# Second gate-up product on VectorE, a load per convolution tap, and a reordered first chunk in a state-space and mixture-of-experts layer

## The reference

```python
h = layernorm(x)
xc, z = split(h @ in_proj_w.T)                    # 2 x 512
u = causal_conv(xc, conv_w) + conv_b              # 4 taps, 512 -> 512 channels
dt = clip(sigmoid(u @ dt_w.T + dt_b), 1e-4, 1.0)
B, C = u @ B_w.T, u @ C_w.T                       # 16 states
state = exp(clip(dt * -exp(A_log), -5, 5)) * state + dt * B * u + 1e-6   # over time
y = sum(state * C) + D * u
x = x + (y * silu(z)) @ out_w.T
h = layernorm(x)
# top 2 of 8 experts by softmax(h @ gate_w.T), weights normalised over the two
x = x + sum_over_picked(w_e * ((silu(h @ Wg_e) * (h @ Wu_e)) @ Wd_e)) \
      + sigmoid(h @ shared_gate) * (silu(h @ Sg) * (h @ Su)) @ Sd       # hidden width 352
```

## Time and profile before

| | us |
|---|---|
| median of 3 runs | 3082.39 |
| lowest and highest | 3077.94, 3083.76 |
| the profiled execution, device time | 3076.53 |
| its span in the trace | 3074.5 |
| busy: TensorE / GpSimd / VectorE / ScalarE | 2651.9 / 2462.9 / 2131.7 / 2115.1 |

### The profile page before, as it was taken

The page is one execution under the profiler, slowest core; times in us unless marked ns, Lnnn a source line. Parts: engine busy times, 40 slices in busy tenths (PEclk is TensorE's granted clock), DMA queues, the critical chain, the costliest instruction groups (busy, mean ns, idle before and its releaser), DMA issues. The chain is left out here.

```text
span 3074.5 us, 57196 instructions
## 1 busy us (share of the span) xinstructions
PE 2651.9 (86%) x15616; PEld 2307.9 (75%) x15616; DVE 2131.7 (69%) x4576; ACT 2115.1 (69%) x4987; POOL 2462.9 (80%) x1667
## 2 busy tenths in 40 slices
PE   6788888898888888988988888889876699999997
PEld 4677877787777777877877777788765577777776
DVE  1889889889888998899899888998894111111111
ACT  1878888888887888888888887888783233333332
POOL 1989999989998999999899988999993365656555
PEclk9889989989988899899898898898987899999999
DMA  3222222223222222222222222222220677777775
GB/s 134 99 70 80 80 73 80 74 75 97 81 77 75 89 73 85 77 74 81 74 79 98 75 76 74 89 74 87 70 70 21 171 184 180 184 177 185 178 184 126
DMA packets 136253, 309.91 MB, mean 101 GB/s; under 512 B 14992, under 2 KB 79632, under 8 KB 135696
## 3 DMA queue, kind: packets, MB, share of 16 engines
q1 hardware_dynamic: 108880, 270.03, 28.0%
q0 software_dynamic: 27072, 36.46, 6.1%
HBM read 258.42 MB, written 48.01 MB: 100 GB/s over the span
## 5 line engine op out<-in xcount | busy, mean ns | idle before, releaser
L1023 POOL TENSOR_TENSOR room<-dtu,b_all 128x1024 f32<-128x1024 f32 x512 | 1202.8, 2368 | 13.3 <-POOL dtu L1000 5.9
L809 ACT ACTIVATE bank<-room,eps_col 128x512 f32<-128x512 f32 x1024 | 693.8, 684 | 309.2 <-DVE carry L1261 213.2
L796 ACT ACTIVATE room<-room,neg_a 128x256 f32<-128x256 f32 x2048 | 868.5, 499 | 9.6 <-DVE room L1247 7.6
L604 PE MATMUL bank<-ident,room 128*128 128x128 f32 x4096 | 556.7, 293 | 239.2 <-DVE room L1256 201.3
L604 PEld LDWEIGHTS bank<-ident,room 128*128 128x128 f32 x4096 | 501.7, 152 | 293.5 <-DVE room L1256 219.5
L1247 DVE TENSOR_TENSOR_SCAN bank<-room,carry,bank 128x256 f32<-128x256 f32 x864 | 580.9, 736 | 61.6 <-ACT bank L809 52.7
L1012 POOL TENSOR_TENSOR room<-room,c_all 128x1024 f32<-128x1024 f32 x224 | 531.8, 2374 | 112.6 <-ACT carry L814 69.2
L1327 DVE SCALAR_TENSOR_TENSOR hid<-hid,bank 128x256 f32<-128x256 f32 (+1 forms) x312 | 131.0, 420 | 631.9 <-ACT up L905 631.9
L1247 DVE TENSOR_TENSOR_SCAN room<-room,carry,bank 128x256 f32<-128x256 f32 x672 | 448.4, 726 | 12.2 <-ACT bank L809 11.5
L1163 POOL DMA_INDIRECT out<-room,ids x144 | 227.7, 1581 | 251.2 <-ACT room L986 221.4
L559 PE MATMUL bank<-xnT,w_conv 128*128 128x256 f32 x3072 | 404.2, 288 | 2.2 <-ACT xnT L832 2.2
(11 more groups left out here) (150 smaller groups left out, 3294.6 us busy)
## 6 DMA issues: line engine op xcount, KB each, us to landing
b_all<-b_scratch SPq DMA_DIRECT2D x128, 512.0 KB, 4.0
c_all<-b_scratch SPq DMA_DIRECT2D x128, 512.0 KB, 5.8
room<-in_wgu SPq DMA_DIRECT2D x72, 704.0 KB, 4.8
room<-in_wd SPq DMA_DIRECT2D x72, 384.0 KB
room<-x_by_expert SPq DMA_DIRECT2D x72, 260.0 KB, 2.7
x_in<-in_x SPq DMA_DIRECT2D x32, 256.0 KB, 5.4
x<-in_x SPq DMA_DIRECT2D x32, 256.0 KB, 2.6
out<-x SPq DMA_DIRECT2D x32, 256.0 KB, 4.2
```

Source lines behind the costliest of these rows:

```text
L604: last = mm(tr_bank[k][:, b * P:(b + 1) * P], v[n % VRING][:, b, k * P:(k + 1) * P], ident[:, :], is_transpose=True, start=False, stop=(n ...
L796: last = af(da[n % RING][:, b, :], dt[c.par][:, b, :], ACT.Exp, scale=neg_a[:, b, n:n + 1])
L809: af(v_slot(n, h)[:, :], v[n % VRING][:, 2 * h:2 * h + 2, :].rearrange("p b t -> p (b t)"), ACT.Identity, bias=eps_col[:, 0:1]).then_inc(v ...
L1023: nc.gpsimd.tensor_tensor(out=v[n % VRING][:, :, :], in0=dtu[:, :, :], in1=row, op=ALU.mult) \
```

## The change

There are three edits. In the diff the parts stand in the order SyncE, TensorE, ScalarE, GpSimd, VectorE.

1. The up half of a gate-up bank is no longer copied by ScalarE nor multiplied by GpSimd. VectorE does both products: first `(tanh + 1) * gate`, then that times up, read from the PSUM bank. It waits for its own first product in between. The buffer `up`, the semaphore `up_ready` and GpSimd's `hidden` are gone. What waited for `up_ready` and `hg_ready` to reuse the bank waits for `h_ready`.
2. The convolution weights are loaded tap by tap, with a semaphore each, behind the x part of the input projection. The four small loads stand behind tap 0 with a semaphore of their own (`w_small`); the first chunk's x comes after them.
3. At the beginning the first chunk's transposes, its copy to `xnT` and the copy's remainder stand before the last of the 8 weight units instead of behind the z weights; the first `dtu` is made by VectorE in two halves; and ScalarE takes the first decay and the first two additions ahead of the rest and of the second chunk's `xnT`.

```diff
-GU_SLOT, GATE_SLOT, HIDDEN_SLOT = [11, 12, 13], [12, 13, 14], [13, 14, 15]
+GU_SLOT, GATE_SLOT = [11, 12, 13], [12, 13, 14]
...
                 def start(self):
...
-                    load_x(Chunk(0, 0))
+                    sp.dma_start(raw_x, wx).then_inc(x_part_loaded, 16)
+                    for t in range(TAPS):
+                        sp.dma_start(raw_conv[:, :, t, :], wconv[:, :, t, :]).then_inc(tap_loaded[t], 16)
+                        if t == 0:
+                            sp.dma_start(a_raw[:, :, :], a_log).then_inc(w_small, 16)
...
+                            load_x(Chunk(0, 0))
                     load_x(Chunk(0, 1))
-                    sp.dma_start(raw_x, wx).then_inc(w_raw, 16)
-                    sp.dma_start(raw_conv, wconv).then_inc(w_raw, 16)
...
             def gate_up(c, u, w, xT, tiled):
...
                 if tiled:
-                    pe.wait_ge(hg_ready, c.index * UNITS + u + HEAD)
-                    pe.wait_ge(up_ready, c.index * UNITS + u + HEAD)
+                    pe.wait_ge(h_ready, c.index * UNITS + u + HEAD)
...
-                    pe.wait_ge(w_raw, 16 * RAW_LOADS)
+                    pe.wait_ge(x_part_loaded, 16)
                     for t in range(TAPS):
+                        pe.wait_ge(tap_loaded[t], 16)
                         for b in range(KM):
+                            n = t * KM + b
+                            if n == TAPS * KM - 1:
...
+                                proj_norm(Chunk(0, 0))
...
                 af(hid[0:rows, hid_slot(c, u), :], bank[0:rows, 0:TC], ACT.Tanh, scale=0.5).then_inc(th_ready, 1)
-                act.wait_ge(h_ready, c.index * UNITS + u + HEAD)
-                af(up[0:rows, (c.par + u) % 2, :], bank[0:rows, TC:2 * TC], ACT.Copy).then_inc(up_ready, 1)
...
                     for slot in range(NS):
                         project(Chunk(0, 0), slot)
+                        if slot == 8:
+                            decays(Chunk(0, 0), 0)
+                    add_eps(Chunk(0, 0), 0, 0)
+                    add_eps(Chunk(0, 0), 0, 1)
+                    decays(Chunk(0, 0), 1)
+                    add_eps(Chunk(0, 0), 1, 0)
+                    decays(Chunk(0, 0), 2)
                     take_normed(Chunk(0, 1))
-                    for n in range(DECAY_LEAD):
-                        decays(Chunk(0, 0), n)
-                    for n, h in ((0, 0), (0, 1), (1, 0)):
-                        add_eps(Chunk(0, 0), n, h)
...
                 def tile(self, t, last):
-                    hidden(counted(t), 0)
-                    hidden(counted(t), 1)
                     if not (t.fixed() and t.index == 0):
                         self.send(t.plus(-1))
-                    hidden(counted(t), 2)
...
                 dve.wait_ge(th_ready, c.index * UNITS + u + 1)
-                dve.wait_ge(up_ready, c.index * UNITS + u + 2 + HEAD)
...
                                            op0=ALU.add, op1=ALU.mult).then_inc(hg_ready, 1)
+                dve.wait_ge(hg_ready, c.index * UNITS + u + 1)
+                vec_e.tensor_tensor(out=h, in0=h, in1=gu_bank(c, u, tiled)[0:rows, TC:2 * TC], op=ALU.mult) \
+                    .then_inc(h_ready, 1)
...
                     for h in range(2):
                         proj_dt(Chunk(0, 0), h)
+                        dve.wait_ge(dt_ready, h + 1)
+                        last = vec_e.tensor_tensor(out=dtu[:, 2 * h:2 * h + 2, :], in0=dt[0][:, 2 * h:2 * h + 2, :],
+                                                   in1=uT[0][:, 2 * h:2 * h + 2, :], op=ALU.mult)
```

More of the change, by code:

```diff
@@ L239, in build @@
         w_early = sem("w_early")
-        w_raw = sem("w_raw")
+        w_small = sem("w_small")
+        x_part_loaded = sem("x_part_loaded")
+        tap_loaded = [sem(f"tap_loaded{t}") for t in range(TAPS)]
         pool_const = sem("pool_const")
@@ L548, in proj_conv @@
                 if half == 0 and j == 0:
-                    shared = c.plus(-3)
-                    wait(pe, hg_ready, units_out(shared, 1))
-                    wait(pe, up_ready, units_out(shared, 1))
+                    wait(pe, h_ready, units_out(c.plus(-3), 1))
                 if half == 1 and j == 0:
@@ L582, in proj_z @@
                 pe.wait_ge(dt_ready, c.index * NT + k + 1)
+                if c.fixed() and c.index == 0:
+                    pe.wait_ge(comp_done, TAPS * KM + 1)
+                    pe.wait_ge(low_done, TAPS * KM + 1)
                 for n, (b, (x_part, w_part)) in enumerate((b, q) for b in range(KM) for q in PASSES):
@@ L713, in start @@
                     pe.sem_inc(dn_ready, 1 + HEAD)
[L714 removed]
+                    pe.wait_ge(x_part_loaded, 16)
                     for t in range(TAPS):
+                        pe.wait_ge(tap_loaded[t], 16)
                         for b in range(KM):
+                            n = t * KM + b
+                            if n == TAPS * KM - 1:
+                                pe.wait_ge(pool_const, 11)
+                                pe.wait_ge(comp_done, 2 + 1)
+                                pe.wait_ge(low_done, 2 + 1)
+                                proj_norm(Chunk(0, 0))
                             for m in range(KD):
[L718 removed]
+                                last = mm(banks[n][:, :], raw_x[:, m, b * P:(b + 1) * P],
                                           raw_conv[:, m, t, :], start=(m == 0), stop=(m == KD - 1))
                             last.then_inc(comp_mm, 1)
[L721 to L723 removed]
+                    pe.wait_ge(comp_done, TAPS * KM)
+                    pe.wait_ge(low_done, TAPS * KM)
                     pe.wait_ge(dve_const, 1)
                     pe.wait_ge(w_early, 16 * EARLY_LOADS)
[L726 removed]
                     for slot in range(NS):
@@ L916, in start @@
                             norm_apply(Chunk(0, 0))
-                        act.wait_ge(comp_mm, n + 1)
+                        if n < TAPS * KM - 1:
+                            act.wait_ge(comp_mm, n + 1)
+                        if n == TAPS * KM - 1:
+                            act.wait_ge(pool_const, 11)
+                            take_normed(Chunk(0, 0))
+                            act.wait_ge(comp_mm, n + 1)
                         af(w_conv[0][:, n // KM, n % KM, :], banks[n][:, :], ACT.Copy).then_inc(comp_done, 1)
+                    act.wait_ge(w_early, 16 * EARLY_LOADS)
                     af(w_z[0][:, :, :], raw_z, ACT.Copy).then_inc(comp_done, 1)
-                    act.wait_ge(pool_const, 11)
                     act.wait_ge(dve_const, 3)
-                    take_normed(Chunk(0, 0))
                     norm_apply(Chunk(0, 1))
@@ L997, in dt_times_u @@
             def dt_times_u(c):
+                if c.fixed() and c.index == 0:
+                    pool.wait_ge(dtu_ready, 1)
+                    return
                 pool.wait_ge(dt_ready, c.index * 2 + 2)
@@ L1058, in scatter @@
                         in_=xn2[c.par][:, k, :], in_offset=None).then_inc(scat_done[c.par], 16)
-            def hidden(c, u):
-                rows = HROWS[u]
-                pool.wait_ge(hg_ready, c.index * UNITS + u + 2 + HEAD)
-                pool.wait_ge(up_ready, c.index * UNITS + u + 2 + HEAD)
-                block_ = hid[0:rows, hid_slot(c, u), :]
-                nc.gpsimd.tensor_tensor(out=block_, in0=block_, in1=up[0:rows, (c.par + u) % 2, :], op=ALU.mult) \
-                    .then_inc(h_ready, 1)
             class Body(Phases):
@@ L1124, in __call__ @@
                             rstd(p_rstd, p_var, p_mv, p_shift, p_var_ready, p_rstd_ready, norm)
-                        if post:
-                            for u in units_of(slot, HIDDEN_SLOT):
-                                hidden(post, u)
                         if post and slot == 13:
@@ L1401, in start @@
                     for n in range(TAPS * KM):
+                        if n == TAPS * KM - 1:
+                            low_normed(Chunk(0, 0))
+                            dve.wait_ge(w_early, 16 * EARLY_LOADS)
+                            vec_e.tensor_scalar_mul(w_bc[:, :, 0:NS], w_bc[:, :, 0:NS], 0.5)
                         dve.wait_ge(comp_done, n + 1)
@@ L1415, in start @@
                     self.flag = dve.value_load(a_flag[0:1, 0:1], min_val=0, max_val=1)
+                    dve.wait_ge(evac, 3)
                     for h in range(2):
                         proj_dt(Chunk(0, 0), h)
+                        dve.wait_ge(dt_ready, h + 1)
+                        last = vec_e.tensor_tensor(out=dtu[:, 2 * h:2 * h + 2, :], in0=dt[0][:, 2 * h:2 * h + 2, :],
+                                                   in1=uT[0][:, 2 * h:2 * h + 2, :], op=ALU.mult)
+                    last.then_inc(dtu_ready, 1)
                     proj_gate(Chunk(0, 0), 0)
```

34 lines of the change are left out of this document (10 added, 24 removed).

## The result

The changed kernel takes 3000.36 us in the median (2997.44 to 3003.31, 4 runs) against 3083.07 (3077.94 to 3087.85) for the kernel before: ratio 0.9732, interval 0.9713 to 0.9751, or 83 us faster. The forecast was 3037, its range ended at 3015. The direction was right; the forecast gain, 45 us, was a little over half of what came.

What follows compares the result with a forecast made beforehand. TensorE was taken to bound the tiles, with waits for GpSimd's product, and three engines to share the chunks. Terms -47 - 4.5 - 0.5 + 20 - 13 = -45 us gave 3037 us, range 3015 to 3062.

Steps and rivals of the forecast that it cites:

- +0.65 us a chunk: Chunks: VectorE's added product, less the shorter waits for ScalarE's copy, lengthens each chunk by 0.65 us, with nothing covering it.
- I count nothing: Chunks: GpSimd has some 2.2 us less work a chunk, but this was given no gain.
- +20: Chunks: 31 chunks at 0.65 us each make the kernel 20 us slower; ends +5 and +35.
- -47: Tiles: without the wait for GpSimd's product the idle time goes and TensorE's groups overlap, -47 us (bounds -35 and -51).
- 10.5 for overlap: Tiles: TensorE's groups overlap by 0.15 us where they follow without a wait, up to 10.5 us over 70 tiles.
- The last tile: End of the tiles: a shorter wait for the product and faster matmuls, -4.5 us (bounds -6 and -2).
- The chain after the last chunk: After the last chunk: the shared expert's down product waits for the same chain once, -0.5 us.
- The sends: Tiles: GpSimd's sends fit narrowly within TensorE's time; as a rival, they bound the tiles, giving 3054 us, chance 0.14.
- the forecast loop of 7.7 to 8.4: Tiles: issue, landing and start-up of GpSimd's sends take 7.7 us, at most 8.4, against TensorE's 8.49 or 8.34.
- Beginning: Start to first scan: earlier weights and convolution give -13 us (bounds -16 and -8), TensorE starting near 9.5.
- -0.4 as taken: Convolution to first scan: taken between -1.6 us for earlier products by B and +1.4 for the second chunk's xnT.
- the fourth rival: Chunks: longer idle time stretches TensorE's slow-clock work, 3099 us at 4 us more a chunk; chance 0.05.

Runs made afterwards that it cites:

- e5: Changed kernel without the second product in the chunks, the first product raising the semaphore itself: 2960.69 us, ratio 0.9612.
- e13: Changed kernel with all chunk relief taken back: ScalarE copies up in place, VectorE waits for it, GpSimd makes a product again: 3036.34 us, ratio 0.9866.
- e10: Changed kernel with an unread 128x256 product on GpSimd in slots 13 to 15 of the chunks: 3006.71 us, ratio 0.9753.
- e1: Kernel before with only the loads by tap and the new order of the first chunk; products as before: 3061.64 us, ratio 0.9941.
- e2: Changed kernel, but in the chunks ScalarE copies up and GpSimd multiplies as before; VectorE makes both products only in the tiles: 2997.98 us, ratio 0.9734.
- e12: Kernel before with only the convolution weights loaded tap by tap: 3069.78 us, ratio 0.9965.
- e3: Changed kernel without the second product in the chunks, VectorE still waiting and raising the semaphore by a separate instruction: 3012.40 us, ratio 0.9782.
- e4: Changed kernel with one more unread VectorE product per unit in the chunks, both operands in SBUF: 3255.06 us, ratio 1.0567.
- e6: Changed kernel with one more unread VectorE product per unit in the chunks, one operand in PSUM: 3025.25 us, ratio 0.9816.
- e8: Changed kernel with ScalarE's tanh ahead of the addition for the next state instead of behind it: 2967.98 us, ratio 0.9641.
- e9: Changed kernel with an unread ScalarE copy of 0.38 us behind each tanh in the chunks: 2998.23 us, ratio 0.9733.
- e11: Changed kernel with one of the two sends of each tile, all waits for landings kept: 2999.15 us, ratio 0.9732.
- e7: Changed kernel, but in the chunks ScalarE copies up to SBUF and VectorE's second product reads that copy: 3252.63 us, ratio 1.0553.
- e14: Kernel with VectorE's second product only in the tiles, and tanh and copy ahead of the addition in ScalarE's slots: 3014.53 us, ratio 0.9795.

## Why the prediction was wrong, step by step

- **Chunks, the failed step.** "+0.65 us a chunk" was the product (1.38) less the shorter waits (0.73). Both parts hold: 1.41 by e5's chunk distance and 0.75 by that of e13 against e10. What failed is the sentence on GpSimd's work, "but nobody waits long for it there; I count nothing". Its relief was worth up to 0.39 us a chunk (e10). The sum 1.41 - 0.75 - 0.39 is +0.27, and the chunk distance grew by 71.02 - 70.78 = +0.24. The traces show where the relief acts. In the mean of 27 chunks the first `gated` starts 52.06 us behind the start of that chunk's `y_tok` in the changed kernel, 52.56 before, and 52.46 with GpSimd's work back (e10). Other kernels fall in the same two groups: 52.47 to 52.68 in e1, e2, e12 and e13, which have that work, 51.81 to 52.08 in e3, e4, e5, e6, e8, e9 and e11, which haven't; e7 (52.43) and e14 (55.23) stand apart, each with a change of its own to this stretch. Which wait hands it on I haven't traced. The distance from the first `gated` to the next `y_tok` grew by 0.74, where the prediction had 0.84. Of the 18 us between +20 and +1.6, GpSimd's relief is up to 12; about 3 are the beginning's gain that comes behind the first scan, and the third distance between chunks (73.9, now 70.5) gave 3.5 by luck. These are the starts of the products for B and C of the fourth and the last chunk, of the kernel before and of after, 28 chunks apart:

```profile
248.44 1.91 PE L577 MATMUL bank<-uT,w_bc 128*32 128x256 f32 x8 [1.42 <-ACT uT L842]
...
2230.37 1.91 PE L577 MATMUL bank<-uT,w_bc 128*32 128x256 f32 x8 [0.93 <-ACT uT L842]
```

```profile
227.27 1.91 PE L577 MATMUL bank<-uT,w_bc 128*32 128x256 f32 x8 [1.54 <-ACT uT L847]
...
2215.88 1.91 PE L577 MATMUL bank<-uT,w_bc 128*32 128x256 f32 x8 [0.93 <-ACT uT L847]
```

- **Tiles, right in mechanism, mis-sized.** -47 was the 37.9 us of idle time in the table of waits and 9 of the 10.5 for overlap. The distance of tiles fell from 9.06 to 8.21, 60 us in 71, beyond the bound of -51. The 37.9 left out the idle time that the table lists under another name (issue): by the windows of the earlier trace rows TensorE was idle 280 - 261.94 = 18.06 us, 0.58 a tile, which is 41 us in 71. The two timelines tell where the rest lay. From the group at 2714.71 to the down product were 2.41 us, now 2706.90 - 2705.17 = 1.73: of the 0.68 only 0.53 stood as idle time, the other 0.15 was the overlap of two groups that follow each other, 11 us in 71. And from the down product to the next group 2.71 went to 2709.50 - 2706.90 = 2.60, since a group behind a wait takes 2.83 to 2.86 itself and one without 2.76; that is 8 us in 71, and I had missed it. The weight loads (LDWEIGHTS) of the down product, before and now, show it: they began with the first matmul at 2717.12, and now begin 0.21 ahead of the one at 2706.90.

```profile
2717.12 2.46 PEld L687 LDWEIGHTS bank<-room,hid 128*128 128x128 f32 x12 [0.93 <-POOL hid L1065]
```

```profile
2706.69 2.57 PEld L687 LDWEIGHTS bank<-room,hid 128*128 128x128 f32 x12
```

The last tile was right: waits 1.42 for 1.4, matmuls 2.83 for 2.86. The chain after the last chunk gave 1.7 for 0.5, too small a sum to matter.
- **The sends.** They fit, as forecast: 8.02 us against the forecast loop of 7.7 to 8.4, and by e11 they are hidden. The landing did get longer, 5.5 us in the median instead of 5.0.
- **Beginning.** -14.6 for -13. TensorE started at 8.16 for 9.5 and the convolution at 39.49 for 41.1. From there to the first scan were 32.96 instead of 33.32, -0.4 as taken, but that was luck. The convolution itself took 11.64 us instead of 13.16, at a granted clock of 1.00 instead of 0.87, which the prediction didn't have (before, then now, columns as in the earlier trace rows):

```profile
53.69:66.85 13.16, 13.15 (x96) 12.95 (x96) 0.82 (x2) 1.93 (x4) 1.03 (x4) 0.87 0.00 1
```

```profile
39.49:51.13 11.64, 11.63 (x96) 11.42 (x96) 2.29 (x6) 2.04 (x5) 1.66 (x5) 1.00 0.01 1
```

TensorE had stood idle for 2.94 and then 1.11 us ahead of it, with the transposes between, now for 1.46. From the end of the convolution to the first scan were 20.16 us, now 21.32: +1.2, since the scan stands behind the second chunk's `xnT` (+1.4 in the prediction), and the earlier products by B gained nothing for it. The start at 8.16 also lies above the 6.6 of the prediction's estimate by the Trainium skill, DMA: Bandwidth & Descriptors, section "Anatomy of one DMA", which is written for transfers issued by GpSimd; these loads are issued by SyncE.
- **The clock.** 0.92 in the window of the chunks for 0.91; the fourth rival didn't occur.
- **Range.** 3015 was too high an end because two terms were wrong in the same direction at once, 18 us in the chunks and 13 in the tiles, which I had thought seldom.

## What to carry to other kernels

A wait in the middle of TensorE's work costs more than its idle time in the table: here 0.85 us a tile for 0.58, since the overlap with the group ahead and the early weight load go too. When work is taken from an engine that is nearly full (GpSimd, 275 of 300 us), count that relief even if no one is seen to wait long for it, and look at what stands ahead of a late operation in its own queue: moving the tanh by one place (e8) gained 28 us. And before a product moves to VectorE, see whether GpSimd is at work, and keep one operand in PSUM.

## What was not expected of the hardware

A VectorE product of 128x256 with both operands in SBUF took 3.03 to 3.05 us in the median and up to 4.84 in the chunks, where GpSimd is busy 8 parts in 10 (e4: 1433 of 1800 us), and 0.42 with one operand in PSUM. An own wait of VectorE followed by a semaphore instruction held it for 0.54 us (e3), an own wait ahead of a product for 0.03 to 0.04.
